# One key chunk's values product in fp16 halves, value projections in the first two row tiles, and a new order of the work between tiles

## The chip, the cores and the metric

The kernel runs on one core of one Trainium2 chip. The metric is the device time of one execution in microseconds (us); lower is better. The core has a matmul engine (TensorE, PE in the rows, with its weight loads apart as PEld), VectorE (DVE), ScalarE (ACT), GpSimd (POOL), and SyncE (SP), which issues transfers. Each runs its own instructions strictly in the order in which they are written and waits for the others by semaphores.

## What is computed

A graph attention layer over 4096 rows of width 128 with two heads, and behind it a mixture of eight small feed-forward experts of which each row uses two. Cut to what matters:

```python
q, k, v = x_ln @ Wq, x_ln @ Wk, x_ln @ Wv            # 4096 x 128, two heads of 64
scores  = einsum('nhd,mhd->hnm', q * SCALE, k)
scores  = where(adj[None] > 0, scores, NEG_INF)      # adj: 4096 x 4096 of 0 and 1
sat     = einsum('hnm,mhd->nhd', softmax(scores), v)
x       = x + leaky_relu(concat(sat[:2048] @ weightr, sat[2048:] @ weightd) + bias)
# then: layer norm, 8 gate scores, top 2, all experts' gelu(x @ W1 + b1) @ W2 + b2, chosen ones added
```

## The kernel before

**Three stages.** The first stage normalises x, transposes it and projects queries, keys and values. The second, the attention, walks over 32 tiles of 128 rows. The third runs the experts over eight chunks of 512 rows. The profile's lines L881 (scores), L896 (transposes) and L912 (values product) are the attention's TensorE work.

**A unit.** For one row tile the 4096 keys are cut into four chunks of 1024, and with two heads this gives eight units, in the order of `UNITS`. For each unit TensorE computes 128 x 1024 scores (fp16 halves, three products); VectorE adds the mask and takes the row minimum (`mask_scores`, L589); ScalarE takes the exponential (L418); TensorE transposes the result back in eight blocks (L896) into one pair of PSUM banks; and ScalarE and VectorE copy that to `pt` in SBUF (L430 and L433, L607). The pair of PSUM banks for transposes exists once: the next unit's transposes wait for these copies. Scores have two such pairs. When both heads of a chunk are copied, `attend` multiplies the chunk's probabilities by the values in fp32 (L912).

**A step.** TensorE's program for step i has four quarters, k = 0 to 3. Each holds the transposes of unit 2k of tile i-1, the scores of units 2k and 2k+1 of tile i, the transposes of unit 2k+1 of tile i-1, and one `attend`. With `AV_BLOCK` = 1 the first quarter's `attend` is the last chunk of tile i-2. The other engines run through the same eight units in their own order. Even and odd steps form a pair, repeated by a loop: in the odd one a pair of finished tiles is projected (`out_project`, k = 1), divided by its sums, put through the leaky ReLU and added to x; in the even one behind it come statistics, normalisation, a transpose (`x2_transpose`, k = 2) and the gate scores (`logits`, k = 3).

**VectorE** does, besides `mask_scores`, half of the copy of each odd unit (`copy_pt`), the small post work, and `make_mask` (L557): the adjacency rows of the next tile, in two halves, turned into 0 or a large negative number behind units 3 and 7.

**GpSimd** issues the adjacency loads (L294), takes two tiny powers, and splits the expert weights into fp16 halves at the beginning of the attention (L305, L307, L309). In the third stage it makes the low halves of the hidden values (L349).

Of the kernel before, what the change touches and what calls it, by code (L numbers as in the profile page):

```python
# [5 lines left out]
F32 = mybir.dt.float32  # L6
# [7 lines left out]
P = 128  # L14
# [27 lines left out]
AV_BLOCK = 1  # L42
# [8 lines left out]
DVE_LOWS = (2, 4, 6)  # L51


def build(nc, x, adj, wq, wk, wv, wr, wd, bias, wg, bg, w1, b1, w2, b2, out):
# [6 lines left out]
    with ExitStack() as ctx:  # L61
# [11 lines left out]
        pt = sb("pt", [P, NU, KT, P], F32)  # L73
# [3 lines left out]
        v_sb = sb("v_sb", [P, NT, D], F32)  # L77
        sat_st = sb("sat_st", [P, PAIR, P], F32)
        o_half = sb("o_half", [P, PAIR, D], F32)
        o_pre = sb("o_pre", [P, PAIR, D], F32)  # L80
        o_act = sb("o_act", [P, PAIR, D], F32)
        x2 = sb("x2", [P, PAIR, D], F32)
# [27 lines left out]
        warm = sb("warm", [P, 1], F32)  # L110
        low = sb("low", [P, HEADS, NP], F32)
# [5 lines left out]
        w1_raw = pt[:, 4:6, :, :].rearrange("p u k q -> p (u k q)")  # L117
        w2_raw = pt[:, 6:8, :, :].rearrange("p u k q -> p (u k q)")
# [5 lines left out]
        xn_t = area(0, 4, 4).rearrange("p (r c) -> p r c", r=4)  # L124
# [51 lines left out]
        pt_by_dve = sem("pt_by_dve")  # L176
        av_done = sem("av_done")
# [3 lines left out]
        post_chain = sem("post_chain")  # L181
        ve2_ready = sem("ve2_ready")
# [31 lines left out]
        def copies_by_dve(j, units):  # L214

            return NU // 2 * j + units // 2
# [13 lines left out]
        W_SPLITS = 13  # L230
# [49 lines left out]
        def _(pool):  # L280
# [5 lines left out]
            pool.memset(expo[:, :], -0.5).then_inc(ones_ready, 1)  # L286

            def load_adj(i, par):

                for c in range(2):  # L290
                    if not isinstance(i, int) or i >= 2:
                        pool.wait_ge(masked, NU * i - 12 + 4 * c)
                    cols = slice(c * HALF, (c + 1) * HALF)
                    pool.dma_start(mask[:, par, cols], adj[bass.ds(i * P, P), cols],  # L294
                                   max_dma_last_dim=8192).then_inc(adj_in[par][c], 16)
# [7 lines left out]
            def split_weights(n, raw, pair):  # L303

                pool.tensor_scalar(raw, raw, W_UP, 0.0, ALU.mult, ALU.add).then_inc(w_split_chain, 1)  # L305
                pool.wait_ge(w_split_chain, 3 * n + 1)
                pool.tensor_scalar(pair[:, 0, :], raw, 1.0, 0.0, ALU.mult, ALU.add).then_inc(w_split_chain, 1)  # L307
                pool.wait_ge(w_split_chain, 3 * n + 2)
                pool.tensor_tensor(pair[:, 1, :], raw, pair[:, 0, :], ALU.subtract).then_inc(w_split_chain, 1)  # L309
# [767 lines left out]
```

## Time and profile before

| | |
|---|---|
| three timed runs | 853.62 us median (851.66 to 853.91) |
| the profiled execution | 851.31 us, of which the span of instructions is 849.5 us |
| TensorE busy | 811.7 us (96%) |
| VectorE busy | 639.2 us (75%) |
| ScalarE busy | 679.0 us (80%) |
| GpSimd busy | 195.5 us (23%) |
| mean granted TensorE clock | 0.989 of full speed |

The busy time is an average over the three stages. In a row of the timeline the first number is the start in us from the start of the span, the second the duration, and what stands in brackets is idle time of the engine before it with what ended it. Rows of several instructions are merged, with their count behind x.

### The profile page before, as it was taken

What the parts mean: (1) busy time and instruction counts of PE and PEld (TensorE: products, weight loads), DVE (VectorE), ACT (ScalarE), POOL (GpSimd) and SP (SyncE); (2) the same over time, 40 slices, a digit from 0 to 9 for tenths busy, and PEclk for the clock granted to TensorE, in tenths of its full rate; (3) what the DMA queues carried; (4) which work ended last, traced back from release to release, by engine and by line L of the source; (5) the groups of instructions that cost most, each with busy time, mean ns of one, the idle gap of its engine ahead of it and who ended that gap; (6) DMA issues with size and microseconds to landing.
All of it is one profiled execution on the core that took longest, in us unless ns stands there. A gap on an engine that the chain in (4) does not pass through costs nothing.

```text
span 849.5 us, 31821 instructions
## 1 busy us (share of the span) xinstructions
PE 811.7 (96%) x12080; PEld 597.7 (70%) x12080; DVE 639.2 (75%) x1530; ACT 679.0 (80%) x1099; POOL 195.5 (23%) x209
## 2 busy tenths in 40 slices
PE   4969999999999999999999999999997889999997
PEld 2537777777777777777777777777776567777775
DVE  6597888888888888888888888887883465555555
ACT  4838887878788888878888888788885789999996
POOL 4180000100100010000001000000000566766774
PEclk9979999999999999999999999999999999999999
DMA  8515433443343334434333443443100000000000
GB/s 220 110 25 91 81 58 58 66 74 58 56 77 59 56 61 72 65 56 69 67 56 58 68 71 56 63 72 56 31 0 2 1 14 14 14 14 12 12 12 12
DMA packets 40900, 44.96 MB, mean 53 GB/s; under 512 B 22168, under 2 KB 32160, under 8 KB 40864
## 3 DMA queue, kind: packets, MB, share of 16 engines
q0 software_dynamic: 9216, 33.56, 24.6%
q1 hardware_dynamic: 31216, 10.71, 5.4%
q8 instruction: 24, 0.39, 0.2%
q10 hardware_dynamic: 432, 0.20, 0.1%
q14 instruction: 12, 0.10, 0.0%
HBM read 71.72 MB, written 2.10 MB: 87 GB/s over the span
## 4 chain that ended last, share of the span: by engine, by line
PE 73%; POOL 14%; issue 8%; DVE 3%; DMA 1%; ACT 0%; POOLq 0%; DVEq 0%
PE ps L912 28%; PE ps L881 19%; PE ps L896 19%; POOL prob L349 14%; PE ps L923 2%; PE ps L837 1%; PE ps L842 1%; PE ps L850 1%; DVE prob L589 1%; PE ps L931 1%; PE ps L828 1%; DMA x_sb<-in_x 1%; DVE stats L513 0%; POOLq L348 0%; ACT prob L418 0%
## 5 line engine op out<-in xcount | busy, mean ns | idle before, releaser
L589 DVE CUSTOM_DVE_ANT_0 prob<-ps,mask 128x1024 f32<-128x1024 f32 x256 | 311.8, 1219 | 90.1 <-PE ps L881 84.4
L418 ACT ACTIVATE prob<-prob,nmax 128x1024 f32<-128x1024 f32 x256 | 292.8, 1144 | 9.9 <-DVE nmax L597 9.9
L912 PE MATMUL ps<-pt,v_sb 128*64 128x128 f32 x4096 | 253.2, 277 | 0.0
L912 PEld LDWEIGHTS ps<-pt,v_sb 128*64 128x64 f32 x4096 | 222.4, 137 | 13.4 <-issue 7.5
L433 ACT ACTIVATE pt<-ps 128x1024 f32<-128x1024 f32 x128 | 131.1, 1024 | 113.0 <-PE ps L896 113.0
L896 PEld LDWEIGHTS ps<-ident,prob 64*128 64x128 f32 x4096 | 152.6, 139 | 78.5 <-issue 78.4
L881 PE MATMUL ps<-k_half,q_row 64*128 64x512 f16 x1536 | 189.7, 380 | 5.0 <-DVE low L589 5.0
L896 PE MATMUL ps<-ident,prob 64*128 64x64 f32 x4096 | 183.7, 229 | 9.4 <-issue 4.7
L349 POOL TENSOR_TENSOR prob<-prob 128x512 f16<-128x512 f32 x104 | 122.6, 1183 | 57.1 <-ACT prob L483 54.4
L294 POOL DMA_DIRECT2D mask<-in_adj x64 | 35.4, 553 | 429.2 <-DVE low L589 429.2
L791 DVE SCALAR_TENSOR_TENSOR x_sb<-ps,k_half,x_sb 128x128 f32 (+1 forms) x256 | 72.5, 344 | 78.1 <-PE ps L1029 76.8
L881 PEld LDWEIGHTS ps<-k_half,q_row 64*128 64x128 f16 x1536 | 71.5, 96 | 68.6 <-issue 9.8
L480 ACT ACTIVATE prob<-ps,b_sb 128x512 f32<-128x512 f32 x128 | 86.9, 679 | 18.3 <-PE ps L1008 16.2
L1027 PE MATMUL ps<-w_pair,prob 128*128 128x128 f16 x512 | 89.9, 220 | 6.6 <-POOL prob L349 4.7
L607 DVE COPY pt<-ps 128x512 f32<-128x512 f32 x128 | 88.0, 688 | 10.8 <-PE ps L896 9.7
L1029 PE MATMUL ps<-w_pair,prob 128*128 128x128 f16 x512 | 89.8, 220 | 0.0
L1028 PE MATMUL ps<-w_pair,prob 128*128 128x128 f16 x512 | 89.8, 220 | 0.0
L483 ACT ACTIVATE prob<-prob 128x512 f16<-128x512 f32 x128 | 80.7, 630 | 4.1
L430 ACT ACTIVATE pt<-ps 128x512 f32<-128x512 f32 x128 | 75.1, 587 | 1.8 <-PE ps L896 1.8
L1027 PEld LDWEIGHTS ps<-w_pair,prob 128*128 128x128 f16 x512 | 50.3, 98 | 14.6 <-POOL prob L349 5.4
L1028 PEld LDWEIGHTS ps<-w_pair,prob 128*128 128x128 f16 x512 | 50.4, 98 | 5.1
L1029 PEld LDWEIGHTS ps<-w_pair,prob 128*128 128x128 f16 x512 | 50.4, 98 | 0.0
(97 smaller groups left out, 670.8 us busy)
## 6 DMA issues: line engine op xcount, KB each, us to landing
mask<-in_adj POOLq DMA_DIRECT2D x64, 512.0 KB, 5.5
q_row<-q_nat SPq DMA_DIRECT2D x128, 32.0 KB, 4.7
x_sb<-in_x SPq DMA_DIRECT2D x4, 512.0 KB, 7.0
out<-x_sb SPq DMA_DIRECT2D x8, 256.0 KB, 2.3
pt<-in_L_ffn_W SPq DMA_DIRECT2D x1, 1024.0 KB, 6.5
wq_sb<-in_L_gnn_Wq ACTq DMA_DIRECT2D x1, 64.0 KB, 2.9
wk_sb<-in_L_gnn_Wk ACTq DMA_DIRECT2D x1, 64.0 KB, 4.5
wv_sb<-in_L_gnn_Wv ACTq DMA_DIRECT2D x1, 64.0 KB, 5.7
```

The source lines that it names most:

```text
L349: pool.tensor_tensor(hid_lo[:, slot, :], hid[:, slot, :], hid_hi[:, slot, :], ALU.subtract).then_inc(hid_lo_ready, 1)
L418: act.activation(prob[:, h, cols], prob[:, h, cols], ACT.Exp, bias=nmax[:, h:h + 1], scale=-1.0, accum_out=sums[:, j, h, p:p + 1]).then_in ...
L433: act.activation(pt[:, u, :, :].rearrange("p k (b q) -> p b k q", b=2), ps[:, TR0:TR0 + 2, :].rearrange("p b (k q) -> p b k q", k=KT), ACT ...
L480: act.activation(hid[:, slot, :], ps[:, (2 * e + b) % UP_BANKS, :], ACT.Gelu, bias=b1_sb[:, e, b:b + 1], scale=1.0 / W_UP).then_inc(hid_ra ...
L589: dve.tensor_tensor_reduce(out=prob[:, h, col_of(p)], in0=ps[:, 2 * (u % 2):2 * (u % 2) + 2, :].rearrange("p b c -> p (b c)"), in1=mask[:, ...
L607: dve.tensor_copy(pt[:, u, :, DH:P], ps[:, TR0 + 1, :].rearrange("p (k q) -> p k q", k=KT)).then_inc(pt_by_dve, 1)
L881: ins = pe.matmul(ps[:, 2 * (u % 2) + half, :], q_row[part, par, h, a, :], k_half[part, h, b, cols], start=first, stop=final)
L896: ins = pe.transpose(ps[:, TR0 + half, t * DH:(t + 1) * DH], prob[part, h, (p * KT + t) * P:(p * KT + t + 1) * P], ident[part, part])
L912: ins = pe.matmul(ps[dims, AV, 0:P], v_sb[:, tile, dims], pt[:, UNITS.index((h, p)), t, :], start=(tile == 0), stop=(tile == NT - 1))
L1027: pe.matmul(bank, hid_hi[:, slot, rows], w2_pair[:, 0, cols], start=(b == 0), stop=False)
L1028: pe.matmul(bank, hid_hi[:, slot, rows], w2_pair[:, 1, cols], start=False, stop=False)
L1029: ins = pe.matmul(bank, hid_lo[:, slot, rows], w2_pair[:, 0, cols], start=False, stop=(b == HB - 1))
```

## The change

**Values product.** For chunk 1 of every tile (`SPLIT_P`, units 1 and 3) the transposed probabilities go to `pt_raw`, GpSimd splits them into an fp16 high part and an fp16 rest, and `attend` takes three fp16 products instead of one fp32 product. The values of that chunk are split once (`split_values`); wv is scaled by 32 and the output weights by 1/32. `AV_BLOCK` becomes 2, so this `attend` stands in the last quarter, and chunks 2 and 3 of a tile are multiplied in the next step.

**Order.** VectorE's half copies are now of units 0, 3, 4 and 7 (`DVE_COPIES`), ScalarE copies units 1, 2, 5, 6 whole. `out_project` moves to k = 2 of the odd step, `divide` behind unit 6, `leaky` behind unit 7; `x2_transpose` moves behind the last `attend` of the even step, `logits` into the next odd step. The residual addition, the variance's epsilon and the normalisation go from VectorE to GpSimd. The expert weights are split in 16 parts, one in each even step.

**Projection of values.** It leaves the first stage: four of its eight chunks are computed in step 0 and four in step 1.

```diff
-AV_BLOCK = 1
+AV_BLOCK = 2
+SPLIT_P = 1
+SPLIT_UNITS = (1, 3)
+V_FIRST = 4
+DVE_COPIES = (0, 3, 4, 7)
...
+            def split_pt(j, u, early=False):
+                q = u // 2
+                pool.wait_ge(pt_by_act, NU * j + u + 1)
+                pool.wait_ge(pt_by_dve, copies_by_dve(j, u + 1))
+                if not early:
+                    pool.wait_ge(av_done, NP * j + SPLIT_P - 3)
...
+                pool.tensor_scalar(pt_hi[:, q, :, :], pt_raw[:, q, :, :], 1.0, 0.0, ALU.mult,
+                                   ALU.add).then_inc(pt_hi_by_pool, 1)
+                pool.wait_ge(pt_hi_by_pool, 2 * j + q + 1)
+                pool.tensor_tensor(pt_lo[:, q, :, :], pt_raw[:, q, :, :], pt_hi[:, q, :, :],
+                                   ALU.subtract).then_inc(pt_by_pool, 1)
...
+                if post and par == 0:
+                    inverse_std(i - 4)
+                    normalise(i - 4)
+                if prior:
+                    if ahead:
+                        pool.wait_ge(mask_ready, 2 * i + 3)
+                    split_pt(i - 1, 1, early)
+                if load:
+                    load_adj(i + 2, par, 0)
+                if prior:
+                    split_pt(i - 1, 3, early)
+                if split and par == 0:
+                    split_ffn_part(i)
+                if load:
+                    load_adj(i + 2, par, 1)
+                if post and par == 1:
+                    residual(i - 3)
...
@@ VectorE's step, the odd half
-                        if u == 1:
+                        if u == 4:
                             invert_sums(i - 3)
-                        if u == 3:
+                        if u == 6:
                             divide(i - 3)
-                        if u == 5:
+                        if u == 7:
                             leaky(i - 3)
-                        if u == 7:
-                            residual(i - 3)
...
@@ TensorE
+                if p == SPLIT_P:
+                    pe.wait_ge(pt_by_pool, 2 * j + 2)
...
+                    if p == SPLIT_P:
+                        for values, probs in ((0, pt_hi), (0, pt_lo), (1, pt_hi)):
+                            for h in range(HEADS):
+                                dims = slice(h * DH, (h + 1) * DH)
+                                ins = pe.matmul(ps[dims, AV, 0:P], v_pair[:, values, t, dims], probs[:, h, t, :],
+                                                start=False, stop=False)
...
+                    if not prior:
+                        project_v(k)
+                    if early:
+                        project_v(V_FIRST + k)
...
-                    if post and par == 1 and k == 1:
+                    if post and par == 1 and k == 2:
                         out_project(i - 3)
```

VectorE in the loop's odd step, from unit 6 to the end of the step, before the change. A unit's `mask_scores` is two rows, L589 and its accumulator; L607 is the copy of unit 7, L597 the row minimum, L557 `make_mask`, L646 the residual addition:

```order
L589 ISA prob,low<-ps,mask 128x1024 [waits post_chain,scores_ready]
L589 ISA low 128x1
L607 COPY pt<-ps 128x8x64 [waits av_done,transposed]
L589 ISA prob,low<-ps,mask 128x1024 [waits scores_ready]
L589 ISA low 128x1
L597 TENSOR_REDUCE nmax<-low 128x1 [waits masked]
L557 TENSOR_SCALAR mask<-mask 128x2048 [waits adj_in01]
L646 ISA
L646 TENSOR_TENSOR x_sb<-x_sb,o_act 128x256
```

And after the change, from unit 6 on, where L692 is `mask_scores`, L735 and L740 are the four instructions of `divide`, L714 is the copy, L658 `make_mask` and L759 `leaky`:

```order
L692 ISA prob,low<-ps,mask 128x1024 [waits scores_ready]
L692 ISA low 128x1
L735 SCALAR_TENSOR_TENSOR o_half<-ps,rinv,bias_b 128x128 [waits o_psum]
L735 SCALAR_TENSOR_TENSOR o_half<-ps,rinv,bias_b 128x128
L740 SCALAR_TENSOR_TENSOR o_pre<-ps,rinv,o_half 128x128 [waits post_chain]
L740 SCALAR_TENSOR_TENSOR o_pre<-ps,rinv,o_half 128x128
L714 COPY pt<-ps 128x8x64 [waits av_done,transposed,post_chain]
L692 ISA prob,low<-ps,mask 128x1024 [waits scores_ready]
L692 ISA low 128x1
L700 TENSOR_REDUCE nmax<-low 128x1 [waits masked]
L658 TENSOR_SCALAR mask<-mask 128x2048 [waits adj_in01]
L759 SCALAR_TENSOR_TENSOR o_act<-o_pre 128x256
```

`divide` now stands between `mask_scores` of unit 6 and the copy of unit 7, and the row behind L759 is the copy of unit 0 of the next step, which before the change was ScalarE's alone.

GpSimd in one odd step, before the change (the second of the two loads of a pair that is in the loop):

```order
L292 ISA
L294 ISA [waits masked]
L294 DMA mask<-in_adj 128x2048
L292 REGISTER_ALU
L294 ISA [waits masked]
L294 DMA mask<-in_adj 128x2048
```

And after the change, where L334 and L337 are the two instructions of `split_pt`, L315 is the load and `pt_hi_by_pool` is a wait for its own first half:

```order
L329 ISA [waits mask_ready]
L330 ISA [waits pt_by_act]
L332 REGISTER_ALU [waits pt_by_dve]
L334 TENSOR_SCALAR pt_hi<-pt_raw 128x1024 [waits av_done]
L336 REGISTER_ALU
L337 TENSOR_TENSOR pt_lo<-pt_raw,pt_hi 128x1024 [waits pt_hi_by_pool]
L313 ISA
L315 ISA [waits masked]
L315 DMA mask<-in_adj 128x2048
L329 REGISTER_ALU
L330 REGISTER_ALU [waits pt_by_act]
L334 TENSOR_SCALAR pt_hi<-pt_raw 128x1024 [waits pt_by_dve,av_done]
```

Where a load stood, two splits now stand behind the wait for `mask_ready` (the first `make_mask` of the step), one on each side of the first load. The second subtraction (L337), the load that waits for unit 7, and the residual addition follow.

TensorE in the last quarter of an odd step, after the change, where L1003 are transposes and L988 scores; before it, the last row's place was taken by L912, which waited for the copies of units 4 to 6 (`pt_by_act`, `pt_by_dve`):

```order
L1003 MATMUL ps<-ident,prob 128x64 [waits pt_by_dve,exp_done,pt_by_act]
L1003 MATMUL ps<-ident,prob 128x64 x15
L988 MATMUL ps<-k_half,q_row 128x512 [waits masked]
L988 MATMUL ps<-k_half,q_row 128x512 x5
L988 MATMUL ps<-k_half,q_row 128x512 [waits masked]
L988 MATMUL ps<-k_half,q_row 128x512 x5
L1003 MATMUL ps<-ident,prob 128x64 [waits pt_by_dve,exp_done,pt_by_act]
L1003 MATMUL ps<-ident,prob 128x64 x15
L1028 MATMUL ps<-pt_hi,v_pair 64x128 [waits pt_by_pool]
```

The last `attend` of a step now waits for GpSimd alone.

## Rows read from the trace of the kernel before

**Rows 1.** Page, part 4: the chain that ended last, by line.

```profile
PE ps L912 28%; PE ps L881 19%; PE ps L896 19%; POOL prob L349 14%; PE ps L923 2%; PE ps L837 1%; PE ps L842 1%; PE ps L850 1%; DVE prob L589 1%; PE ps L931 1%; PE ps L828 1%; DMA x_sb<-in_x 1%; DVE stats L513 0%; POOLq L348 0%; ACT prob L418 0%
```

**Rows 2.** Busy time by stretch: the steady attention, header and row.

```profile
core 0: us, PE busy (x) PEld busy (x) DVE busy (x) ACT busy (x) POOL busy (x), PEclk, DMA share, GB/s
95.00:595.00 500.00, 500.00 (x8298) 375.86 (x8296) 419.19 (x897) 406.74 (x656) 38.34 (x66) 1.00 0.39 64
```

**Rows 3.** The chain in order of time: two products one pair of steps apart.

```profile
300.19 1.90 PE ps L912 x32
...
337.54 1.90 PE ps L912 x32
```

**Rows 4.** Timeline, last quarter of an odd step: start, duration, engine, line.

```profile
330.44 0.71 PE L896 MATMUL ps<-ident,prob 64*128 64x64 f32 x16
...
330.59 0.41 DVE L640 SCALAR_TENSOR_TENSOR o_act<-o_pre 128x256 f32<-128x256 f32 x1
...
331.19 1.02 ACT L433 ACTIVATE pt<-ps 128x1024 f32<-128x1024 f32 x1 [0.65 <-PE ps L896]
331.95 1.22 DVE L589 CUSTOM_DVE_ANT_0 prob<-ps,mask 128x1024 f32<-128x1024 f32 x1 [0.95 <-PE ps L881]
...
332.32 0.71 PE L896 MATMUL ps<-ident,prob 64*128 64x64 f32 x16
...
332.96 1.97 PE L912 MATMUL ps<-pt,v_sb 128*64 128x128 f32 x32
...
333.10 0.69 DVE L607 COPY pt<-ps 128x512 f32<-128x512 f32 x1
...
333.70 1.21 DVE L589 CUSTOM_DVE_ANT_0 prob<-ps,mask 128x1024 f32<-128x1024 f32 x1
...
334.86 0.71 PE L896 MATMUL ps<-ident,prob 64*128 64x64 f32 x16
...
335.03 0.69 DVE L557 TENSOR_SCALAR mask<-mask 128x2048 bf16<-128x2048 bf16 x1
```

**Rows 5.** Timeline, second quarter of the same step: projection, mask preparation, division.

```profile
322.99 1.13 PE L923 MATMUL ps<-wrd,sat_st 128*128 x4
...
324.87 0.69 DVE L557 TENSOR_SCALAR mask<-mask 128x2048 bf16<-128x2048 bf16 x1
325.48 0.60 DVE L628 SCALAR_TENSOR_TENSOR o_half<-ps,rinv,bias_b 128x128 f32<-128x128 f32 x2
...
326.12 0.61 DVE L633 SCALAR_TENSOR_TENSOR o_pre<-ps,rinv,o_half 128x128 f32<-128x128 f32 x2
```

**Rows 6.** Timeline near 45 us: GpSimd's weight splits and VectorE's mask preparations.

```profile
44.74 4.07 POOL L309 TENSOR_TENSOR w_pair<-pt,w_pair 128x2048 f16<-128x2048 f32 x1
...
46.85 2.50 DVE L557 TENSOR_SCALAR mask<-mask 128x2048 bf16<-128x2048 bf16 x1
```

**Rows 7.** Groups by line: GpSimd's splits, long and short, and its load.

```profile
L309 POOL TENSOR_TENSOR w_pair<-pt,w_pair 128x2048 f16<-128x2048 f32 x2 | 8.1, 4074 | 0.2
...
L294 POOL DMA_DIRECT2D mask<-in_adj x64 | 35.4, 553 | 429.2 <-DVE low L589 429.2
...
L307 POOL TENSOR_SCALAR w_pair<-pt 128x2048 f16<-128x2048 f32 x2 | 3.8, 1898 | 0.2
...
L309 POOL TENSOR_TENSOR wg_pair<-wg_sb,wg_pair 128x8 f16<-128x8 f32 x1 | 0.2, 202 | 0.1
```

**Rows 8.** Timeline of the experts: fp16 products of 128 columns, three starts apart.

```profile
666.44 0.23 PE L1027 MATMUL ps<-w_pair,prob 128*128 128x128 f16 x1 [4.04 <-POOL prob L349]
...
666.62 0.22 PE L1027 MATMUL ps<-w_pair,prob 128*128 128x128 f16 x1
```

**Rows 9.** Timeline of the first stage: ScalarE's copies of x, then the next projection.

```profile
27.14 1.08 ACT L376 ACTIVATE prob<-ps 128x512 f32<-128x512 f32 x2
...
29.16 1.88 PE L837 MATMUL ps<-prob,wq_sb 128*128 128x512 f32 x4
```

**Rows 10.** Timeline of the last step: TensorE behind the ranking of gates.

```profile
640.25 0.72 PE L896 MATMUL ps<-ident,prob 64*128 64x64 f32 x16 [2.07 <-DVE pt L607]
```

More of the change, by code:

```diff
@@ new lines, in step @@
+            def step(i, par, prior=True, post=True, ahead=True, load=True, split=True, early=False):
+                if post and par == 0:
[15 more added lines that the diff above has]
+                    residual(i - 3)
@@ L312, in _ @@
+            pool.wait_ge(ones_ready, 3)
+            pool.wait_ge(qkv_w_in, 16 * N_QKV_W)
+            pool.tensor_scalar(wv_sb[:, :], wv_sb[:, :], V_UP, 0.0, ALU.mult, ALU.add).then_inc(wv_scaled, 1)
             for i in range(X_PARTS):
                 inverse_std_x(i)
-            load_adj(0, 0)
-            load_adj(1, 1)
-            pool.wait_ge(k_lo_ready, NC)
+            for i in range(2):
+                for c in range(2):
+                    load_adj(i, i, c)
+            step(0, 0, prior=False, post=False, split=False)
@@ L343, in ffn @@
+            step(2, 0, post=False)
+            step(3, 1)
+            pairs(pool, 4, NT - 2, step)
+            step(NT - 2, 0, load=False)
+            step(NT - 1, 1, load=False, ahead=False)
+            step(NT, 0, load=False, ahead=False, split=False)
+            inverse_std(NT - PAIR)
             def ffn(j, par):
@@ L410, in _ @@
                     normalise_x(2 * p + 5)
+            for j in range(V_FIRST - 1):
+                copy_v(j)
             def exp_unit(j, u):
@@ L457, in _ @@
             step(0, prior=False)
+            copy_v(V_FIRST - 1)
             step(1, early=True)
@@ L460, in _ @@
             step(3)
-            pairs(act, 4, NT, lambda i, par: step(i, post=par == 0))
-            step(NT, now=False, post=True, last=True)
+            step(4)
+            step(5, post=True)
+            pairs(act, 6, NT, lambda i, par: step(i, post=par == 1))
+            step(NT, now=False, last=True)
+            x2t_high(NT - 2 * PAIR)
             act.wait_ge(b1_in, 16)
@@ L580, in _, with mask_scores @@
             low_qk(3)
-            def mask_scores(i, par, u):
+            def mask_scores(i, par, u, prior):
                 h, p = UNITS[u]
+                if u % 2 and u not in DVE_COPIES and prior:
+                    dve.wait_ge(transposed, NU * i - NU + u + 1)
                 if u in (0, 4):
@@ L971, in _ @@
             pe.wait_ge(w_split_chain, W_SPLITS)
-            step(3, 1)
-            pairs(pe, 4, NT, step)
+            step(3, 1, ready=False)
+            step(4, 0)
+            step(5, 1)
+            pairs(pe, 6, NT, step)
             step(NT, 0, now=False)
-            for p in range(NP - AV_BLOCK, NP):
-                attend(NT - 1, p)
+            attend(NT - 1, NP - 2)
+            logits(NT - 2 * PAIR)
+            attend(NT - 1, NP - 1)
+            pe.wait_ge(w_split_chain, W_SPLITS + 3 * (NT - PAIR))
             def gate_transpose(j):
```

255 lines of the change are left out of this document (154 added, 101 removed).

## The prediction

> **What bounds the kernel now.** I read the chain that ended last first: three quarters of the span lie on TensorE, 28% on the values product, 19% on the scores, 19% on the transposes [rows 1]. The table by stretch says how firmly: from 95 to 595 us TensorE is busy 500 us of 500, at the full granted clock, while VectorE has 419 and ScalarE 407 [rows 2]. So in the steady attention every us that TensorE saves is a us of the kernel, and every us that it waits is a new one. The chain in order of time gives the beat: the same product comes at 300.19 and at 337.54, so a pair of steps takes 37.35 us [rows 3], and there are 15 such pairs (steps 2 to 31). The reader should then look at one quarter of a step instead of at the averages: in the last quarter of an odd step TensorE starts its first transposes at 330.44, the second ones at 332.32, the product at 332.96, and the next quarter at 334.86 [rows 4]. VectorE's mean of 84% hides that its work comes in an order; what counts is whether the copy that frees the one pair of PSUM banks for transposes is done in time.
>
> **The product in fp16.** The fp32 product holds TensorE from 332.96 to 334.86, 1.90 us [rows 4]. In its place come 8 blocks x 3 products x 128 columns, with the two heads side by side in different columns of the array as before. Three fp16 products of 128 columns start within 666.44 to 666.62, 60 ns each with the rounding [rows 8]. 24 x 0.056 to 0.060 is 1.34 to 1.44 us, and the entry and exit that the fp32 block has too (1.90 less its columns) adds some 0.1: I take 1.48. The lower end is 1.35; the upper is 1.90, no gain, if the 48 separate weight loads set the pace. Gain 0.42 us a step, 0.84 a pair.
>
> The trace has no column-tiled fp16 product with its own weights each time. The Trainium skill (TensorEngine Tiling (Array Packing), Feature Incompatibilities) says that column tiling excludes the fast weight load, and TensorE: Matmul & The Clock Gate (LDWEIGHTS) gives columns divided by 1.2 GHz, 53 ns for 64 columns. If the two heads' loads ran one after the other that would be 48 x 53 ns, an estimate of 2.6 us instead of 1.48; no row here shows it, and 16 loads of 128 columns in fp32 inside a 0.71 us group of transposes [rows 4] speak against it.
>
> **Copies.** In the first half of a quarter ScalarE copies a whole unit in 1.02 us, ending at 332.21, and the second transposes follow 0.11 later [rows 4]: they wait for the copy. Units 0 and 4 are now copied in halves, which frees them until TensorE's own work ends; at most 0.1 us each, taken 0.07, in three places of a pair (the fourth is lost below): 0.21 us a pair.
>
> **GpSimd in between.** `split_pt` twice: GpSimd's 2048 wide operations took 1.898 us (one input) and 4.074 us (two inputs), an 8 wide one 0.202 [rows 7], so 1024 columns cost 1.05 and 2.13. With 0.085 between two dependent ones a split is 3.27 us. Behind the mask preparation stand 0.15 of signal, 3.27, the load's 0.55 [rows 7], 3.27 and 0.1 back to TensorE: 7.35 us. What TensorE leaves for it: in the odd step the preparation ends at 325.56 [rows 5] and the last product starts at 332.96 [rows 4], 7.40 us, and `out_project` still stands between the two after the change. That just fits. In the even step nothing stands there any more (`x2_transpose` and `logits` move out), so it is shorter by the projection's 1.06 (1.13 less its overlap [rows 5]): 6.34 us. TensorE waits 1.0 us in every even step. Bounds: 0.5, if the load and the gaps hide; 1.7, if GpSimd's register work stands beside each wait.
>
> **VectorE at the odd step's end.** This is the largest term, and no busy share shows it. `divide` costs 1.25 us (325.48 to 326.73 [rows 5]). Before, it stood behind a mask preparation, where the next copy was far off. Now it stands between `mask_scores` of unit 6 and the copy of unit 7. Laid over [rows 4]: unit 6 starts at 331.95, and the row behind it can start at 333.10; the division, with the wait for its own end, takes until 334.40; the copy of unit 7 (0.69) until 335.09, so TensorE's next transposes start at 335.15, where the shorter product would have allowed 332.96 + 1.48 = 334.44. **Wait 0.7 us.** Then, in program order and each beginning in the tail of the one before: `mask_scores` of unit 7 from 335.00; `make_mask` 1.33 behind it at 336.33 (before, that distance was 333.70 to 335.03, the row minimum in it [rows 4]); `leaky` 0.6 behind, at 336.93, for 0.41 [rows 4]; and only from 337.30 to 337.99 the copy of unit 0, which ScalarE did alone before. TensorE's second transposes want it 1.88 us behind the first, at 337.03, and get it at 338.05. **Wait 1.0 us.** Queued behind that copy are `mask_scores` of units 0 and 1 and the statistics; the following quarter has room for them. The even step's end has no division and no `leaky`, and fits. Moving the residual, the epsilon and the normalisation to GpSimd relieves VectorE by 1.2 us a pair, but elsewhere.
>
> **Sum for a pair.** -0.84 -0.21 +1.0 +0.7 +1.0 = +1.65 us; 15 pairs: **+24.8 us**. Bounds of the terms together: +1.0 to +2.5 a pair.
>
> **The beginning.** In a round of the first stage ScalarE ends its copies of x at 28.22 and the next projection starts at 29.16 [rows 9]; the value projection between them goes, 0.9 us in each of three rounds, with the end of the last one some 3.0 us. VectorE's mask preparation took 2.50 us instead of 0.69 while GpSimd's subtraction of 4.07 us ran, and ended just behind it [rows 6]; the same meets the next preparation, beside the second such subtraction. The expert weights are now split later in small pieces, so 1.8 and an estimated 2.8 us go. Against that the value projections come back in steps 0 and 1, 3.6 us in the latter and some 0.5 of the former not hidden, plus ScalarE's copy of them, 0.6; and step 1 has one product less (-1.9), paid at the end. Together -4.8 us; bounds -8 and -1.
>
> That the preparation stands behind GpSimd agrees with the Trainium skill (GPSIMD Engine Reference, Key points): the two share SBUF interfaces when VectorE is in a two-port mode. It is also why the wait for `mask_ready` is there at all.
>
> **The end.** The ranking of gates held VectorE's copy, and TensorE stood 2.07 us [rows 10]; it is now ranked one copy later, with fewer copies of its own in the way. About -2.1 us for that gap and an estimated -2.0 for the two shorter quarters behind it, +1.9 for the product that moved: -2.2 us, bounds -4 and +2.
>
> **Total.** 24.8 - 4.8 - 2.2 = +17.8 us. Against the profiled execution, 851.31 us (1.8 of it outside the span), that is 869.1; the median of the timed runs lies 2.3 us above that execution, so for a median the change's size on top of 853.62 gives 871.4; I settle between the two, at 870.5.
>
> **Rivals.** (A) *VectorE absorbs the division.* If the copies of units 7 and 0 came in time, a pair would be -0.84 -0.21 +1.0 = 0, and only the ends would be left: 853.6 - 7 = 846.6 us, faster than before. The point where it decides is the budget from unit 6's `mask_scores` to the copy of unit 0: TensorE leaves 334.44 + 1.88 - 331.95 = 4.4 us, the list above needs 6.0 (331.95 to 337.99). For it: VectorE is only 84% busy; against it: strict order. (B) *Everything hides*, GpSimd too: -1.05 x 15 - 7 = -23, 831 us. Against it: 7.35 against 6.34. (C) *The fp16 product gains nothing*, so the change does not do what it says: 0.42 x 31 = 13 us more, less what the same waits then cover (0.3 a pair): 878 us. (D) *GpSimd is slower than its rows* beside VectorE's masks, or its small weight pieces hold the even step's second mask preparation (at most 0.43 each): +0.7 a pair, 881 us. (E) *One of the two VectorE waits only*: 857 us.
>
> **Chances.** Forecast 0.56 (861 to 880 by itself), A 0.13, B 0.06, C 0.08, D 0.08, E 0.09. A measurement of this kernel can tell some 0.3% from no change, 2.6 us. Faster than that: A, B, 0.18. Within: the edges of A and E, 0.05. Slower: 0.77. The range leaves out B and the greater part of A: 848 to 886.
>
> **What would show it.** In the profile after, the steady stretch has TensorE with 2.7 us of idle time a pair, in three places: before the fp16 product in even steps, released by GpSimd's subtraction (1.0 us); before the first and before the second transposes of an even step, released by VectorE's copies (0.7 and 1.0 us). The fp16 product holds TensorE 1.5 us. A pair takes 39.0 us. If those copies' waits are missing, A is right; if the product's wait is missing in even steps, GpSimd was over-priced; if the product takes 1.9 us, C. The first product would start about 5 us closer to the beginning, counted by steps. What would make the forecast wrong altogether is one mistake in the list of VectorE's order at the odd step's end, since more of the loss hangs on it than on any other term.

## The result

| | before | after |
|---|---|---|
| median of the timed runs (4 and 4) | 852.99 us | 877.51 us (875.00 to 877.94) |
| the profiled execution, and its span | 851.31, 849.5 us | 875.0, 873.3 us |
| TensorE, VectorE, ScalarE, GpSimd busy | 811.7, 639.2, 679.0, 195.5 us | 793.2, 624.7, 683.3, 463.6 us |

The changed kernel is slower: ratio 1.0283, 95% interval [1.0258, 1.0308]. TensorE does 18.5 us less and the kernel takes 24 us more, so some 42 us of new idle time stand on TensorE. All that follows is read in spans (873.3 against 849.5, +23.8 us).

The chain that ended last, by engine and by line, answers to [rows 1], where three quarters were TensorE's:

```profile
PE 48%; POOL 22%; issue 15%; DVE 11%; POOLq 1%; ACT 1%; DMA 1%; DVEq 1%
PE ps L1033 14%; POOL prob L440 13%; PE ps L988 13%; PE ps L1003 12%; POOL pt_lo L337 4%; DVE prob L692 4%; POOL pt_hi L334 4%; PE ps L1028 3%; DVE pt L714 2%; PE ps L1045 2%; DVE mask L658 1%; PE ps L944 1%; POOL mask L315 1%; DVE o_half L735 1%; PE ps L949 1%
```

GpSimd and VectorE now hold a third of it. The 13% at L440 are GpSimd's part in the experts, which was there before as 14% at L349; new are the splits (L334, L337), the load and VectorE's rows. The steady stretch, header and row (start:end, then busy time with instruction counts), answers to [rows 2]:

```profile
core 0: us, PE busy (x) PEld busy (x) DVE busy (x) ACT busy (x) POOL busy (x), PEclk, DMA share, GB/s
...
107.00:595.00 488.00, 450.52 (x8096) 342.72 (x8094) 379.85 (x784) 381.68 (x608) 255.37 (x287) 1.00 0.37 60
```

TensorE was busy 500 of 500 us; now 37.5 of 488 are idle, at the same full clock. What it waited for, over the whole kernel (total us, times, longest; the two largest entries of its attention):

```profile
PE ps L1028 <- POOL pt_lo L337: 28.0, 29, 1.6
PE ps L1003 <- DVE pt L714: 18.5, 31, 1.6
```

L1028 is the fp16 product, L1003 the transposes. In the timeline of one pair of steps (TensorE, only the rows that waited) they are:

```profile
303.31 0.72 PE L1003 MATMUL ps<-ident,prob 64*128 64x64 f32 x16 [0.19 <-DVE pt L714]
...
306.18 0.71 PE L1003 MATMUL ps<-ident,prob 64*128 64x64 f32 x16 [0.85 <-DVE pt L714]
...
321.61 0.25 PE L1028 MATMUL ps<-pt_hi,v_pair 128*64 128x128 f16 x2 [1.55 <-POOL pt_lo L337]
...
340.91 0.25 PE L1028 MATMUL ps<-pt_hi,v_pair 128*64 128x128 f16 x2 [0.47 <-POOL pt_lo L337]
```

Four waits, 3.06 us a pair. The pair runs from the odd step's product at 301.59 to the one at 340.91: 39.3 us, where [rows 3] had 37.35.

Where the 23.8 us lie, by the starts of a tile's first scores (tile 2 to tile 31 is 14.5 pairs):

| stretch | before | after | difference |
|---|---|---|---|
| start of the span to the scores of tile 2 | 74.9 | 69.7 | -5.2 |
| tile 2 to tile 31 | 540.5 | 567.7 | +27.3 |
| tile 31 to the last values product | 42.2 | 43.5 | +1.2 |
| from there to the end (experts) | 192.0 | 192.5 | +0.5 |

### The profile page after: what moved, and what is told of

The parts are those of the page before. It is cut to its first block, busy times and chain, and to the rows that moved or that the text cites. A ratio compares the mean times of both kernels' runs of the same rounds, so it can differ in the third digit from the quotient of the medians.

```text
span 873.3 us, 33539 instructions
## 1 busy us (share of the span) xinstructions
PE 793.2 (91%) x12592; PEld 588.2 (67%) x12592; DVE 624.7 (72%) x1469; ACT 683.3 (78%) x1099; POOL 463.6 (53%) x494
## 4 chain that ended last, share of the span: by engine, by line
PE 48%; POOL 22%; issue 15%; DVE 11%; POOLq 1%; ACT 1%; DMA 1%; DVEq 1%
PE ps L1033 14%; POOL prob L440 13%; PE ps L988 13%; PE ps L1003 12%; POOL pt_lo L337 4%; DVE prob L692 4%; POOL pt_hi L334 4%; PE ps L1028 3%; DVE pt L714 2%; PE ps L1045 2%; DVE mask L658 1%; PE ps L944 1%; POOL mask L315 1%; DVE o_half L735 1%; PE ps L949 1%
## 5 line engine op out<-in xcount | busy, mean ns | idle before, releaser
L692 DVE CUSTOM_DVE_ANT_0 prob<-ps,mask 128x1024 f32<-128x1024 f32 x256 | 312.0, 1221 | 113.1 <-PE ps L988 104.6
L1003 PEld LDWEIGHTS ps<-ident,prob 64*128 64x128 f32 x4096 | 152.4, 138 | 81.8 <-issue 80.7
L1003 PE MATMUL ps<-ident,prob 64*128 64x64 f32 x4096 | 180.5, 227 | 24.2 <-DVE pt L714 18.5
L1033 PE MATMUL ps<-pt,v_sb 128*64 128x128 f32 x3072 | 190.5, 277 | 0.0
L988 PE MATMUL ps<-k_half,q_row 64*128 64x512 f16 x1536 | 187.7, 376 | 1.9 <-DVE k_half L651 1.5
L1033 PEld LDWEIGHTS ps<-pt,v_sb 128*64 128x64 f32 x3072 | 167.2, 138 | 10.5 <-issue 5.1
L334 POOL TENSOR_SCALAR pt_hi<-pt_raw 128x1024 f16<-128x1024 f32 x64 | 67.1, 1049 | 181.1 <-DVE mask L658 174.0
L440 POOL TENSOR_TENSOR prob<-prob 128x512 f16<-128x512 f32 x104 | 122.6, 1183 | 57.3 <-ACT prob L584 54.6
L337 POOL TENSOR_TENSOR pt_lo<-pt_raw,pt_hi 128x1024 f16<-128x1024 f32 x64 | 137.0, 2141 | 5.3
L526 ACT ACTIVATE pt<-ps 128x1024 f32<-128x1024 f32 x96 | 98.3, 1024 | 42.9 <-PE ps L1003 42.6
L988 PEld LDWEIGHTS ps<-k_half,q_row 64*128 64x128 f16 x1536 | 72.5, 95 | 62.5 <-issue 7.1
L523 ACT ACTIVATE pt<-ps 128x512 f32<-128x512 f32 x96 | 56.9, 593 | 73.3 <-PE ps L1003 73.3
L714 DVE COPY pt<-ps 128x512 f32<-128x512 f32 x96 | 65.8, 686 | 27.0 <-PE ps L1003 26.5
L315 POOL DMA_DIRECT2D mask<-in_adj x64 | 39.0, 610 | 81.2 <-DVE low L692 78.2
L1028 PE MATMUL ps<-pt_hi,v_pair 128*64 128x128 f16 x1024 | 49.0, 220 | 28.0 <-POOL pt_lo L337 28.0
```

Of the source, the lines that this page charges most:

```text
L334: pool.tensor_scalar(pt_hi[:, q, :, :], pt_raw[:, q, :, :], 1.0, 0.0, ALU.mult, ALU.add).then_inc(pt_hi_by_pool, 1)
L337: pool.tensor_tensor(pt_lo[:, q, :, :], pt_raw[:, q, :, :], pt_hi[:, q, :, :], ALU.subtract).then_inc(pt_by_pool, 1)
L440: pool.tensor_tensor(hid_lo[:, slot, :], hid[:, slot, :], hid_hi[:, slot, :], ALU.subtract).then_inc(hid_lo_ready, 1)
L526: act.activation(to.rearrange("p k (b q) -> p b k q", b=2), ps[:, TR0:TR0 + 2, :].rearrange("p b (k q) -> p b k q", k=KT), ACT.Copy).then_ ...
L692: dve.tensor_tensor_reduce(out=prob[:, h, col_of(p)], in0=ps[:, 2 * (u % 2):2 * (u % 2) + 2, :].rearrange("p b c -> p (b c)"), in1=mask[:, ...
L988: ins = pe.matmul(ps[:, 2 * (u % 2) + half, :], q_row[part, par, h, a, :], k_half[part, h, b, cols], start=first, stop=final)
```

## The experiments

The theory: the loss is four waits at known places, each the end of a list that one engine works off in strict order, and not the amount of work. The rivals: the amount of work on VectorE or GpSimd sets the pace; or a removed wait is replaced by the next one. Every ratio below is against the kernel before on the same chip; two chips were used, and the median of the kernel before lay between 852.3 and 853.2 us throughout. "Pair" is the mean distance between the same scores of two steps, from tile 4 to tile 30.

### Without the division

```diff
-                        if u == 6:
-                            divide(i - 3)
```

This leaves out the division of the 15 pairs in the loop; the one for the last pair stays. Not shown: `o_pre` is set to zero once ahead of the attention, and `leaky` gives the signals that the division gave.

> The changed kernel without the division of the 15 pairs inside the loop: o_pre stays zero, so the attention's share of x is left out there (the last pair keeps it); everything else runs. Theory: the 1.25 us behind unit 6 are what makes the copies of units 7 and 0 late; both waits (0.19 and 0.96 us a pair) go, some 1.1 us a pair, 17 us in all: 860 us. Rival (VectorE has room, only GpSimd's splits cost): less than 3 us, 875 to 877 us.

Measured: 860.01 us, ratio 1.0076 [1.0058, 1.0095], pair 38.15 us. As the theory said. Both waits for the copies are gone, those for GpSimd stand at 1.54 and 0.47 us as before. So the division's place costs 1.14 us a pair in this kernel, where the prediction had 1.7 for VectorE; the reason that it gave against rival A, strict order, holds.

### The same division, one unit earlier

```diff
-                        if u == 6:
+                        if u == 5:
                             divide(i - 3)
-                        if u == 7:
                             leaky(i - 3)
```

> Only the division and the leaky ReLU one unit earlier, GpSimd's order as in the changed kernel. Theory (the VectorE waits come from where the division stands, not from its work): the same as the kernel that leaves the division out, 858 to 862 us. Rival (VectorE's total work sets it, 72% busy): no change from 875, since the work stays.

Measured: 861.20 us, ratio 1.0091 [1.0074, 1.0107]. The pair is 38.32 us. The work is back, and nearly all of the gain stays: no wait for VectorE's copies is left in the pair, and the wait for GpSimd in odd steps is 0.64 us instead of 0.47. It was the place and not the amount of work. The place was to be seen in the changed kernel's trace, VectorE in the odd step:

```profile
339.36 1.22 DVE L692 CUSTOM_DVE_ANT_0 prob<-ps,mask 128x1024 f32<-128x1024 f32 x1 [2.02 <-PE ps L988]
...
340.51 0.60 DVE L735 SCALAR_TENSOR_TENSOR o_half<-ps,rinv,bias_b 128x128 f32<-128x128 f32 x2
341.15 0.61 DVE L740 SCALAR_TENSOR_TENSOR o_pre<-ps,rinv,o_half 128x128 f32<-128x128 f32 x2
341.79 0.69 DVE L714 COPY pt<-ps 128x512 f32<-128x512 f32 x1
```

VectorE stands idle for 2.02 us ahead of unit 6, with the projection that the division needs finished at 336.02, and then divides where a copy is wanted. `divide` and `leaky` together are 1.7 us and fit the gap.

### Other units copied in halves

```diff
-DVE_COPIES = (0, 3, 4, 7)
+DVE_COPIES = (1, 3, 5, 7)
```

> The changed kernel with one thing put back: VectorE's half copies are of units 1, 3, 5 and 7 again, so unit 0 is ScalarE's alone. My theory: TensorE's wait of 0.96 us a pair before the second transposes of an even step hangs on VectorE's list (unit 7's mask, row minimum, make_mask, leaky, copy of unit 0) and goes; nothing else moves. A pair of steps goes from 39.3 to 38.4 us and the time from 877.5 to about 864 us. Rival: that wait only follows from the late fp16 product, ScalarE comes no earlier, and the time stays within 3 us of 877.

Measured: 876.42 us, ratio 1.0279 [1.0262, 1.0296], pair 39.08. The theory missed. The time is the rival's, but not its reason: the wait is gone. (The 0.96 us of the expectation is 0.85 in the rows above.) The three largest entries of TensorE's waits in the attention, over this whole kernel:

```profile
PE ps L1028 <- POOL pt_lo L337: 22.7, 28, 1.4
PE ps L1003 <- DVE pt_raw L714: 9.6, 16, 2.9
PE ps L1003 <- DVE pt L714: 6.2, 15, 0.8
```

And its timeline at the beginning of an even step:

```profile
305.75 0.49 DVE L749 BATCH_NORM_STATS2 stats<-x_sb 128x6 f32 x2
...
306.60 0.69 DVE L714 COPY pt_raw<-ps 128x512 f32<-128x512 f32 x1
...
307.44 0.71 PE L1003 MATMUL ps<-ident,prob 64*128 64x64 f32 x16 [0.38 <-DVE pt_raw L714]
```

The wait for the copy of unit 0 is gone, but unit 1's copy now stands behind the statistics and comes 0.38 us late, unit 7's is 0.35 late instead of 0.19, and the four waits of the pair add up to 2.35 us instead of 3.06. The pair falls by only 0.2, so 0.5 us of that were given back outside any wait. The starts in the two traces show where: in the quarters k = 0 and k = 2, in which units 0 and 4 are copied whole again. One of them in this run:

```profile
312.40 1.46 PE L988 MATMUL ps<-k_half,q_row 64*128 64x512 f16 x12
313.81 0.71 PE L1003 MATMUL ps<-ident,prob 64*128 64x64 f32 x16
314.45 1.97 PE L1033 MATMUL ps<-pt,v_sb 128*64 128x128 f32 x32
```

From the scores to the product are 2.05 us here and 1.88 in the changed kernel with its half copies (313.69 to 315.57), in three such quarters of a pair without a late copy: 0.5 us. The last step lost too: VectorE's ranking of the gates holds the copy of unit 3, TensorE waits 2.88 us for it (the 2.9 above), and the stretch behind tile 31 took 45.3 us instead of 43.5.

### GpSimd's load behind both splits

```diff
-                if load:
-                    load_adj(i + 2, par, 0)
                 if prior:
                     split_pt(i - 1, 3, early)
+                if load:
+                    load_adj(i + 2, par, 0)
```

> The changed kernel with GpSimd's first adjacency load put behind the second split. It takes 0.64 us and its gaps out of the chain from the mask preparation to the fp16 product. Theory: the even step's wait falls from 1.6 to 0.9 us, the odd one's 0.5 goes, but then VectorE's copy of unit 7 is late by its own 0.5 to 0.7 instead of 0.2: net 0.9 to 1.1 us a pair, 862 to 865 us. Rival (the product waits for something else, such as the copies): no change, 877 us.

Measured: 866.69 us, ratio 1.0173 [1.0152, 1.0193], pair 38.64. The rival (no change) falls; the gain of 0.65 us a pair is smaller than the 0.9 to 1.1 of the theory, and the time lies 1.7 us above its range. TensorE's waits in one pair of this kernel, all of them:

```profile
300.22 0.71 PE L1003 MATMUL ps<-ident,prob 64*128 64x64 f32 x16 [0.73 <-DVE pt L714]
303.08 0.71 PE L1003 MATMUL ps<-ident,prob 64*128 64x64 f32 x16 [0.86 <-DVE pt L714]
317.85 0.25 PE L1028 MATMUL ps<-pt_hi,v_pair 128*64 128x128 f16 x2 [0.85 <-POOL pt_lo L337]
```

Where GpSimd isn't late, the copy of unit 7 is late by 0.73 us: the 0.7 of the prediction, which GpSimd's own lateness had covered in the changed kernel. The waits for GpSimd fell by 1.17 us a pair, and 0.54 came back in this way.

### The first split ahead of the mask preparation

```diff
+                if prior:
+                    split_pt(i - 1, 1, early)
                 if post and par == 0:
                     inverse_std(i - 4)
                     normalise(i - 4)
                 if prior:
                     if ahead:
                         pool.wait_ge(mask_ready, 2 * i + 3)
-                    split_pt(i - 1, 1, early)
-                if load:
-                    load_adj(i + 2, par, 0)
-                if prior:
                     split_pt(i - 1, 3, early)
+                if load:
+                    load_adj(i + 2, par, 0)
```

> GpSimd makes the fp16 halves of unit 1 as soon as they are copied, ahead of its wait for the mask preparation, so that only unit 3 (3.3 us) is left behind that wait, and the adjacency load goes behind both. Theory (the product's waits come from the length of the chain behind the mask wait): both product waits of a pair (1.55 + 0.47) go; the copies of units 7 and 0 wait for VectorE as with the load last (0.73 + 0.86 = 1.59 in place of 1.04), so a pair is 39.3 - 2.02 + 0.55 = 37.8 and the whole 875 - 1.47 x 15 = 853 us. Rival (the collision with VectorE's mask preparation comes back through the first split, which runs where nothing was before): a preparation grows by 1 to 3 us and a pair is 39 or more, 870 us or over.

Measured: 853.31 us, ratio 1.0014 [1.0003, 1.0025], pair 37.70. As the theory said: no wait for GpSimd is left, 0.73 and 0.86 us for the copies are. So GpSimd's part of the loss was not its 7.7 us of work but that all of it stood behind one wait, though unit 1's probabilities had been there since the quarter before. The load was moved too; by itself (the run before) it gave 11 of the 24 us.

### Both moves

The division and `leaky` behind unit 5, and the first split ahead of the wait: the two edits above in one kernel.

> The early split of the run before, and VectorE's division and leaky ReLU one unit earlier, behind the row maximum of unit 5, where VectorE is idle for 2.02 us in the changed kernel's trace. Theory (every microsecond over the old pair is one of the four waits, and none has a successor): pair 39.3 - 3.06 = 36.2 to 36.5, the whole 829 to 833 us, faster than the kernel before by 2.3 to 2.8%. Rival (a removed wait is replaced by the next one within a few tenths, as with the moved copies): pair 37.3 or more, 846 us or over.

Measured: 830.15 us (830.07 to 831.03), ratio 0.9736 [0.9720, 0.9752], pair 36.07. The theory's number; the timeline names no wait of TensorE in the pair. Each product and each scores group follows at TensorE's own pace, here in the chain in order of time (L1032 is the fp32 product, L1027 the fp16 one, L987 the scores):

```profile
301.37 1.46 PE ps L1027 x48
...
315.68 1.90 PE ps L1032 x32
318.23 1.29 PE ps L987 x12
320.10 1.46 PE ps L1027 x48
...
337.42 1.46 PE ps L1027 x48
```

301.37 to 337.42 is 36.05 us. All work of the changed kernel is in it, in another order. Here and below the edits shift the line numbers by a few.

### Chunk 1 in fp32 again

Two kernels: the changed one with chunk 1's product in fp32 and no splits on GpSimd, and that one with the division one unit earlier too. The product then waits for the copies as the other chunks' does (not shown).

```diff
-                        for values, probs in ((0, pt_hi), (0, pt_lo), (1, pt_hi)):
-                            for h in range(HEADS):
-                                ... v_pair[:, values, t, dims], probs[:, h, t, :]
+                        for h in range(HEADS):
+                            ... v_sb[:, tile, dims], pt_raw[:, h, t, :]
```

> The changed kernel with chunk 1 multiplied in fp32 again and no splitting by GpSimd; order, copies and the other moves stay. Theory: GpSimd's waits go (1.6 us in the even and 0.5 us in the odd step), the product is 0.42 us longer twice, VectorE's waits stay: a pair 39.3 - 2.1 + 0.85 = 38.0 us, in all 858 us, still slower than the 853 of before the whole change. Rival (the whole loss is the splits'): below 850 us, since the beginning gains 5 us.

Measured: 859.63 us, ratio 1.0079 [1.0062, 1.0095], pair 38.15. As the theory said.

> Chunk 1's product in fp32 as in the kernel before (no splits on GpSimd), with the division one unit earlier; what is left of the change is the value projections in the first tiles. Theory: pair 38.15 - 1.12 = 37.03, the whole 857.7 + 1.9 - 16.8 = 842 to 844 us, 1.1% under the kernel before; the run with both splits and division moved should then be 11 to 13 us below this one, which is the fp16 product's own gain (0.42 x 31). Rival (fp16 with its 48 weight loads gains nothing where nothing waits): the two are within 2 us.

Measured: 837.41 us, ratio 0.9819 [0.9803, 0.9836], pair 36.69. Five us below the theory, since the pair without waits is 0.66 us shorter than before and not 0.3. Where they come from is what the moved copies showed: four quarters of a pair, 0.17 us each. Both kernels with moved division side by side give the fp16 product's own worth: 36.69 - 36.07 = 0.62 us a pair, 7.3 us in the medians. The rival (under 2 us) falls, but the theory's 11 to 13 us were too much: the product is 0.44 us shorter, and the even step keeps all of it; but in the odd step the next transposes start 1.62 us behind the product's start (320.03 to 321.65) where 1.46 would do, and the quarter behind them is 0.12 longer, since VectorE's copies are only just in time there. That the whole is 7.3 and not 15 x 0.62 = 9.3 or more led to the next run: the stretch behind tile 31 took 44.1 us in fp16 and 40.0 in fp32.

### The ranking of gates two units later

In the last step VectorE ranks the gates while GpSimd now makes a split. The kernel with both moves, VectorE and GpSimd:

```profile
613.51 1.04 POOL L334 TENSOR_SCALAR pt_hi<-pt_raw 128x1024 f16<-128x1024 f32 x1 [5.84 <-ACT pt_raw L526]
613.96 0.83 DVE L801 TENSOR_TENSOR k_half<-logit,k_half 128x224 f32<-128x224 f32 x1
...
614.64 2.15 POOL L337 TENSOR_TENSOR pt_lo<-pt_raw,pt_hi 128x1024 f16<-128x1024 f32 x1
614.71 2.32 DVE L802 TENSOR_TENSOR k_half<-logit,k_half 128x224 f32<-128x224 f32 x1
...
617.49 2.40 DVE L805 TENSOR_TENSOR k_half<-k_half 128x28 f32<-128x28 f32 x7
...
619.93 0.69 DVE L714 COPY pt_raw<-ps 128x512 f32<-128x512 f32 x1
```

In the kernel before, whose GpSimd was idle at that time, the same three groups took 0.39, 0.38 and 1.69 us. The second of them:

```profile
636.74 0.38 DVE L696 TENSOR_TENSOR k_half<-logit,k_half 128x224 f32<-128x224 f32 x1
```

In the fp32 kernel they took 0.39, 0.80 and 1.69; there the last operation of GpSimd's normalisation (0.80 us) ran beside the second. The 0.80 of the expectation below is therefore not the comparison alone. Here the groups hold the copy of unit 3, TensorE waits 2.30 us for it, and then works 4.7 us at half the clock. Its wait in the timeline:

```profile
620.88 0.72 PE L1002 MATMUL ps<-ident,prob 64*128 64x64 f32 x16 [2.30 <-DVE pt_raw L714]
```

And busy time by stretch (columns as above):

```profile
618.00:622.60 4.60, 1.31 (x30) 0.99 (x25) 3.34 (x8) 1.57 (x4) 2.92 (x4) 0.89 0.00 0
622.60:627.30 4.70, 4.70 (x50) 4.25 (x50) 0.00 (x0) 2.91 (x5) 1.43 (x1) 0.50 0.00 0
```

```diff
-                    if last and u == 2:
+                    if last and u == 4:
                         rank_gates(0, 0, RANKED_EARLY)
```

> The kernel with the early split and the early division, and in the last step the ranking of gates two units later, behind the copy of unit 4. Theory (in the last step the ranking's two-input operations stretch beside GpSimd's split, 0.80 to 2.32 us and 0.39 to 0.83, and hold the copy of unit 3: TensorE waits 2.3 us and then runs 4.4 us of work at half clock): the stretch from the last tile's scores to the attention's end falls from 44.0 to some 40.5 us, the whole from 830 to 826 or 827. Rival (the ranking only moves the wait to the copy of unit 7): no change.

Measured: 827.23 us (825.92 to 828.21), ratio 0.9700 [0.9687, 0.9713]. The stretch behind tile 31 fell from 44.1 to 39.2 us, 1.3 more than the theory said, and the granted clock stays at 1.00 there. The whole fell by 2.9 us only: in these two profiles the scores of tile 2 came 0.8 us later and the experts took 1.1 us longer, which is within what kernels with the same code in these stretches show (69.6 to 71.2, and 192.3 to 193.4 us). This is the fastest version: 3.0% under the kernel before, 5.7% under the changed one (827.23 against 877.51).

### GpSimd without its wait for the mask preparation

```diff
-                    if ahead:
-                        pool.wait_ge(mask_ready, 2 * i + 3)
```

Once on the changed kernel, once on the one with both moves.

> The changed kernel with GpSimd's wait for the mask preparation taken out, nothing else. Theory: the fp16 product finds its halves ready (the 28 us of waits for GpSimd go), but VectorE's preparation is held by the splits, and the waits for VectorE's copies grow by 1 to 2 us a pair beyond the 1.6 that stand without GpSimd's: 865 to 880 us, so little or nothing is gained over 875. Rival (the wait costs and brings nothing): the same as with the first split ahead of the wait, 853 us.

Measured: 861.51 us, ratio 1.0108 [1.0091, 1.0124], below the theory's range and above the rival's number; pair 38.17. VectorE's preparation (L656) in the even step, beside the subtraction of the first split, and what came of it:

```profile
306.82 2.15 POOL L337 TENSOR_TENSOR pt_lo<-pt_raw,pt_hi 128x1024 f16<-128x1024 f32 x1
...
308.27 1.25 DVE L656 TENSOR_SCALAR mask<-mask 128x2048 bf16<-128x2048 bf16 x1
...
310.46 0.71 PE L1001 MATMUL ps<-ident,prob 64*128 64x64 f32 x16 [0.23 <-DVE pt L712]
```

The collision is real, 1.25 us instead of 0.69. The wait that it leads to is 0.23 us, but the copies behind it come late for the product too: from the scores to the product of this quarter are 2.33 us instead of 1.88. That is 0.45 of the 0.47 us by which the pair is longer than with the first split ahead of the wait (37.70), and most of the 8 us between the two times. The wait that was to prevent it cost the changed kernel 16 us (877.51 against 861.51), because the splits queued up behind it.

> The same kernel as with the early split and the early division, with GpSimd's wait for the mask preparation taken out: the split of unit 3 starts as soon as its copies are made. Theory (VectorE's mask preparation is held until a running GpSimd operation ends): in the odd step the preparation falls into the 2.13 us subtraction, takes over 1.5 us instead of 0.69, and the copy of unit 4 behind it comes late; TensorE waits some 1.3 us a pair, 845 to 850 us in place of 830. In the even step the normalisation keeps the split behind the preparation, nothing changes. Rival (the wait is caution only): 830 us, preparations of 0.7 us throughout.

Measured: 831.42 us, ratio 0.9749 [0.9734, 0.9764], not to be told from 0.9736 [0.9720, 0.9752] with the wait. The theory missed. The odd step shows why:

```profile
312.15 1.04 POOL L334 TENSOR_SCALAR pt_hi<-pt_raw 128x1024 f16<-128x1024 f32 x1 [0.87 <-DVE pt_raw L712]
...
312.97 0.76 DVE L656 TENSOR_SCALAR mask<-mask 128x2048 bf16<-128x2048 bf16 x1
...
313.27 2.45 POOL L337 TENSOR_TENSOR pt_lo<-pt_raw,pt_hi 128x1024 f16<-128x1024 f32 x1
```

The preparation starts beside the conversion, not beside the subtraction, 0.3 us earlier than that, and loses 0.07 us; the subtraction that starts beside it loses 0.31. The expectation had placed it at least 0.3 us too late, in a list where that decides.

## Why the prediction was right, and where its terms were off

It said 870.5 us (848 to 886), slower; the median is 877.5. The change was put at 17.8 us and is 24.5 (medians) or 23.8 (spans). Step by step:

**What bounds it.** Right. Every wait that the trace names came out as time of the kernel: 3.06 us of waits a pair over a pair without waits of 36.07 makes 39.13, and 39.29 was measured. (One of the four quarters with half copies has the late copy in it and loses its 0.17 us.)

**The product, 1.48 us.** Right: 1.46 to 1.53 in the chain for the 48 products. If weight loads set a pace, it was not that of rival C (1.90) nor the 2.6 us of the two-loads-in-a-row reading; both fall. The gain a pair was 0.62 us, not 0.84, where both forms run without waits.

**The copies, 0.21 us a pair.** Too small. The fp32 kernel with the moved division has a pair of 36.69 against 37.35, so 0.66 us come from the new copies and order. The starts of TensorE's groups show it in the quarters k = 0 and 2: the second transposes follow the scores after 1.29 us instead of 1.41, and the product follows the transposes after 0.59 instead of 0.64, four times a pair. The prediction read its 0.1 us in a quarter k = 3 [rows 4], where the distance is 1.33 us before and after, and where nothing was to be gained. Together with the product the pair without waits was predicted at 36.30 and is 36.07.

**GpSimd, 7.35 us.** Here is the mis-sized term. In the trace after, GpSimd from the preparation's end to the product:

```profile
313.19 0.69 DVE L658 TENSOR_SCALAR mask<-mask 128x2048 bf16<-128x2048 bf16 x1
...
314.30 1.04 POOL L334 TENSOR_SCALAR pt_hi<-pt_raw 128x1024 f16<-128x1024 f32 x1 [3.76 <-DVE mask L658]
315.43 2.14 POOL L337 TENSOR_TENSOR pt_lo<-pt_raw,pt_hi 128x1024 f16<-128x1024 f32 x1
317.52 0.64 POOL L315 DMA_DIRECT2D mask<-in_adj  x1
318.19 1.06 POOL L334 TENSOR_SCALAR pt_hi<-pt_raw 128x1024 f16<-128x1024 f32 x1
319.33 2.13 POOL L337 TENSOR_TENSOR pt_lo<-pt_raw,pt_hi 128x1024 f16<-128x1024 f32 x1
```

The operations cost what the wide ones of [rows 7] gave, 1.05 and 2.14. The load took 0.60 to 0.64 instead of 0.55, and its register work and the signals cost 0.42 ahead of the first split where 0.15 had been put: 313.88 to 321.61 is 7.73 us. TensorE left less than the list had: 6.18 us in the even step (7.73 less the wait) instead of 6.34, which is the 0.17 by which a quarter with half copies is shorter. TensorE waited 1.55 us in even steps and 0.47 in odd ones, not 1.0 and 0. "That just fits" for the odd step was 7.35 against 7.40; a margin of 0.05 us between two lists that are both estimated is no margin. This term is 1.0 us a pair too small.

**VectorE at the odd step's end, 0.7 and 1.0.** The list and its order were right: from `mask_scores` of unit 6 to the end of unit 0's copy are 6.00 us (300.04 to 306.04), 6.04 predicted. It was not the largest term in this kernel: 1.04 us a pair against GpSimd's 2.02. Measured 0.19 and 0.85 in the changed kernel, 0.73 and 0.86 where GpSimd isn't late. I added the two engines' waits as if they were independent; 0.5 us of VectorE's lie under GpSimd's. That the pair came out near is in part luck, since the two errors work against each other (GpSimd 1.0 too small, VectorE 0.7 too large): waits of 2.7 predicted, 3.06 measured; pair 39.0 predicted, 39.3 measured. Of the +24.8 for 15 pairs +27.3 came, in the 14.5 pairs of the table.

**The beginning, -4.8.** Measured -5.2, with the first scores 3.17 us earlier (38.05 for 41.22) and both preparations back at 0.69 and 0.68 us where [rows 6] had 2.50 for the first. The second, which was estimated, stands in the trace of before beside a subtraction of 4.08 us that ends at 57.25:

```profile
54.28 3.53 DVE L557 TENSOR_SCALAR mask<-mask 128x2048 bf16<-128x2048 bf16 x1
```

So 1.8 and 2.8 us went, as put. The total is right to about 1.5 us and no better: among the runs with the same first steps the scores of tile 2 start between 69.6 and 71.2 us. No run took the parts of this term separately.

**The end, -2.2.** Wrong: +1.2. The ranking does come one copy later, but GpSimd's split of the last tile is now beside it, which the prediction didn't look at. In the changed kernel the seven small operations at L805 took 3.97 us, the wait behind the ranking is 1.11 us instead of the 2.07 of [rows 10]; and ahead of it TensorE waits 0.84 and 1.55 us for the two copies behind the division, and then runs one fp32 product in 3.57 us instead of 1.97, at a granted clock of 0.53. The kernel before had the same behind its 2.07 us, a product of 3.53 us; so the stretch at half the clock didn't go but moved:

```profile
658.39 0.71 PE L1003 MATMUL ps<-ident,prob 64*128 64x64 f32 x16 [1.55 <-DVE pt L714]
659.03 3.57 PE L1033 MATMUL ps<-pt,v_sb 128*64 128x128 f32 x32
...
663.20 3.97 DVE L805 TENSOR_TENSOR k_half<-k_half 128x28 f32<-128x28 f32 x7
...
668.15 0.71 PE L1003 MATMUL ps<-ident,prob 64*128 64x64 f32 x16 [1.11 <-DVE pt_raw L714]
```

No run moved the ranking in the changed kernel itself; in the kernel with both moves the same edit was worth 4.9 us of this stretch.

**The rivals.** A (VectorE absorbs the division) and B (everything hides) were states that this work can reach and this order doesn't. Moving the division alone, which is A's condition, gives 861 us and not A's 846.6, since GpSimd's waits are 2.2 us a pair there and not 1.0; the early split alone gives 853, both together 830, B's 831. C fell with the product's time. Of D the second half was there, a preparation of 0.87 us beside the small weight pieces (322.06), but no wait of TensorE follows it; its first half was not, since the splits took what their rows gave. E would have been one VectorE wait; there were two.

## What to carry to other kernels

When the bounding engine has no idle time left, price a change by writing out, for each engine that feeds it, the list of instructions between two of its deadlines, and compare its length with what the bounding engine leaves; a busy share of 72% does not tell it. Waits of two engines on the same path need not add (0.73 us shrank to 0.19 behind a late product), and a margin of a few hundredths is a coin toss. Before giving up a change that loses in this way, look for an idle gap of the late engine ahead of the deadline and for work that stands behind a wait it doesn't need: two such moves turned +2.8% into -2.6%, a third made it -3.0%.

## What the runs showed of the hardware

VectorE and GpSimd hold each other up in more forms than the mask preparation of [rows 6]. A VectorE comparison of 224 elements with two fp32 inputs took 2.32 us beside a GpSimd subtraction of 2.15 us and 0.80 beside a shorter GpSimd operation, against 0.38 alone. Seven operations of 28 elements took 1.69 us alone, and 2.40 and 3.97 us in the two kernels in which GpSimd worked beside some of them. A bf16 preparation of 2048 elements took 1.25 us instead of 0.69 when it began 1.45 us into the subtraction, and 0.76 when it began within the one-input conversion; the GpSimd subtraction beside that one took 2.45 instead of 2.14. The prediction had priced the preparation alone.

TensorE's granted clock fell to 0.50, the lower of its two levels (1.2 GHz), for 4.7 us of unbroken work behind a stretch of 4.6 us in which it was busy for 1.31; so a late copy in the last step cost 2.3 us of waiting and about as much again behind it, 4.9 us in all when the ranking was moved.
